# Q and k turned by VectorE blocks and SBUF moves instead of TensorE, with the row tiles in another order

## The reference

```
q, k = rmsnorm(xn @ Wq) * q_w, rmsnorm(xn @ Wk) * k_w      # per head, over its 128 columns
scores = q @ k.T / sqrt(128) - slope[h] * distance         # causal
y = rmsnorm(softmax(scores) @ v) * sub_w
out = x + concat(y) @ Wproj + fp8_roundtrip(xn) @ W8.T
```

## Time and profile before

| what | value |
|---|---|
| median of 3 runs (lowest to highest) | 547.68 us (547.47 to 548.8) |
| the profiled execution: its time, its span | 549.33 us, 547.2 us |
| TensorE matmul, busy | 521.6 us, 95% |
| VectorE, ScalarE, GpSimd, busy | 417.8, 391.6, 333.9 us |
| share of TensorE in the chain that ended last | 86% |
| mean of the DMA engines | 20 GB/s |

### The profile page before, as it was taken

One profiled execution on the slowest core, in us unless ns is written; L12 is line 12 of the kernel. 1 busy time (PEld: TensorE's weight loads), 2 busy tenths in 40 slices (PEclk: granted clock), 3 DMA queues, 4 the chain that ended last, 5 costly groups with the idle time before them and its releaser, 6 DMA issues.

```text
span 547.2 us, 11863 instructions
## 1 busy us (share of the span) xinstructions
PE 521.6 (95%) x3420; PEld 481.4 (88%) x3420; DVE 417.8 (76%) x1031; ACT 391.6 (72%) x887; POOL 333.9 (61%) x430
## 2 busy tenths in 40 slices
PE   6678999999999999999999999999999999999985
PEld 2667899999999999999999999999999999999874
DVE  5876768777787867878787777878678787868775
ACT  2367878686876968677696868768686877868662
POOL 3385587574758737676576748587376856747221
PEclk9699999999999999999999999999999999999999
DMA  5200100101010010101001010100101000000002
GB/s 158 58 2 1 40 1 1 40 2 40 2 38 0 0 38 0 38 0 38 0 1 37 0 38 0 38 0 9 30 0 38 0 10 0 10 2 1 2 1 77
DMA packets 18581, 10.81 MB, mean 20 GB/s; under 512 B 2176, under 2 KB 18560, under 8 KB 18560
## 3 DMA queue, kind: packets, MB, share of 16 engines
q1 hardware_dynamic: 17568, 10.49, 6.6%
q10 hardware_dynamic: 992, 0.07, 0.1%
HBM read 9.51 MB, written 1.05 MB: 19 GB/s over the span
## 4 chain that ended last, share of the span: by engine, by line
PE 86%; DVE 5%; ACT 4%; issue 2%; DMA 1%; POOL 1%; POOLq 0%; DVEq 0%; SPq 0%
PE pT_ps L562 11%; PE qkv_ps L477 10%; PE qkv_ps L479 8%; PE qkv_ps L478 8%; PE yT_ps L479 7%; PE yT_ps L478 7%; PE yT_ps L477 7%; PE score_big L477 5%; PE score_big L478 4%; PE score_big L479 4%; PE misc L538 3%; PE score_small L479 2%; PE score_small L478 2%; PE score_small L477 2%; ACT stage L734 1%
## 5 line engine op out<-in xcount | busy, mean ns | idle before, releaser
L919 DVE TENSOR_TENSOR pT_lo<-pT_ps,pT_hi 128x384 fp32r<-128x384 f32 (+1 forms) x192 | 101.0, 554 | 41.9 <-ACT pT_hi L762 41.2
L734 ACT ACTIVATE stage<-qkv_ps 128x384 f32<-128x384 f32 x119 | 58.5, 492 | 83.0 <-PE qkv_ps L479 82.3
L754 ACT ACTIVATE probs<-probs,neg_max 128x1024 f32<-128x1024 f32 (+7 forms) x128 | 98.4, 770 | 16.8 <-DVE neg_max L910 16.7
L762 ACT ACTIVATE pT_hi<-pT_ps 128x384 fp32r<-128x384 f32 (+1 forms) x192 | 86.2, 484 | 17.4 <-PE pT_ps L562 12.6
L431 POOL TENSOR_TENSOR y_r<-y_ms,minus_half 128x4 f32<-128x4 f32 x32 | 32.7, 1022 | 105.8 <-DVE y_ms L938 105.8
L477 PE MATMUL qkv_ps<-w_hi,xT_hi 128*128 128x384 f32 x242 | 87.9, 363 | 2.6 <-ACT stage L734 0.6
L562 PE MATMUL pT_ps<-ident,probs 128*128 128x128 f32 x576 | 84.5, 274 | 4.2 <-ACT probs L754 3.5
L478 PE MATMUL qkv_ps<-w_lo,xT_hi 128*128 128x384 f32 x242 | 82.0, 339 | 0.0
L479 PE MATMUL qkv_ps<-w_hi,xT_lo 128*128 128x384 f32 x242 | 81.9, 338 | 0.0
L391 POOL TENSOR_TENSOR qk_r<-qk_ms,minus_half 128x4 f32<-128x4 f32 x64 | 64.8, 1013 | 27.2 <-DVE qk_ms L884 25.6
L562 PEld LDWEIGHTS pT_ps<-ident,probs 128*128 128x128 f32 x576 | 66.3, 141 | 9.2 <-ACT probs L754 4.4
(11 more groups left out here) (183 smaller groups left out, 1313.3 us busy)
## 6 DMA issues: line engine op xcount, KB each, us to landing
w_raw<-in_wq SPq DMA_DIRECT2D x16, 128.0 KB, 2.2
w_raw<-in_wk SPq DMA_DIRECT2D x16, 128.0 KB, 2.3
w_raw<-in_wv SPq DMA_DIRECT2D x16, 128.0 KB, 2.3
wp_raw<-in_wproj SPq DMA_DIRECT2D x16, 128.0 KB, 2.1
acc<-in_x SPq DMA_DIRECT2D x2, 512.0 KB, 5.5
out<-acc SPq DMA_DIRECT2D x8, 128.0 KB, 1.8
w<-in_ffn_w ACTq DMA_DIRECT2D x1, 64.0 KB, 6.8
q_col<-in_q_w ACTq DMA_DIRECT2D x1, 0.5 KB, 2.9
```

Source lines behind the costliest of these rows:

```text
L734: act.activation(stage_of(h, k // 2)[:, k % 2, :], qkv_bank(h, k)[:, 0:3 * D], ACT.Copy).then_inc(qkv_read, 1)
L754: act.activation(probs[:, s % 2, 0:(i + 1) * P], probs[:, s % 2, 0:(i + 1) * P], ACT.Exp, bias=neg_max[:, par, s:s + 1], scale=-1.0, accum ...
L762: act.activation(pT_hi[g][:, a:b, r * P:(r + 1) * P], pT_ps[(CHUNK0[s] + k) % 2][:, 0:(b - a) * P].rearrange("p (j t) -> p j t", t=P), ACT ...
L919: dve.tensor_tensor(pT_lo[g][:, a:b, r * P:(r + 1) * P], pT_ps[(CHUNK0[s] + k) % 2][:, 0:(b - a) * P].rearrange("p (j t) -> p j t", t=P), ...
```

## The change: what it does

TensorE's `transpose_qk` goes for the heads 1 to 15. For each pair VectorE turns every 32x32 block of `qk_n` in place (`turn_blocks`, one instruction over 128x512, into `turned`), and SP moves the blocks to where a full transpose has them: 16 transfers within SBUF (`move_qk`), each 32 partitions by 128 columns (16 KB), into `qk_raw`. `qk_hi` and `qk_lo` then read `qk_raw` in SBUF rather than PSUM, and `qk_lo` has three instructions instead of two. `turned` and `qk_raw` have two buffers each: `turn_blocks` waits until the moves of two pairs ago have landed, and `move_qk` until `qk_lo` of two pairs ago is done. Head 0 still uses TensorE.

The row tiles go in the order 3, 4, 2, 5, 1, 6, 0, 7, so that a head's first score needs two of its four pairs, the second three, and only the sixth all (`NEEDS`). `qk_hi` and `qk_lo` of pair 3 move into step 1 of the head itself. The calls of all engines are placed anew: each `turn_blocks` stands one step or so behind its `mean_squares`, `qk_lo(k)` comes two or three steps later (turn 0, 1, 2, 3 in steps 1, 3, 5, 7; lo 0, 1, 2 in steps 4, 5, 7; lo 3 in step 1 of the next head); `project(h + 2, 0)` is pulled into the end of head h; GpSimd does `norm_qk` ahead of its weight splits. The far parts of `pT_hi` and `pT_lo` become narrower.

In the prologue x comes in four loads, `dist` is built before the normalization, `split_w(1, 1)` waits until x is normalized, ten more warm-up matmuls stand behind the first transposes, the first projections start with half of x, and the decoding of the fp8 weights is spread over the steps of head 0. The last head's closing calls are reordered.

```
-    ORDER = [7, 0, 6, 1, 5, 2, 4, 3]
+    ORDER = [3, 4, 2, 5, 1, 6, 0, 7]
...
+    WIDE = 4
+
+    NEEDS = [max(ORDER[:s + 1]) // 2 + 1 for s in range(NT)]
...
+            def move_qk(h, k):
+
+                m = NPAIR * (h - 1) + k
+                sp.wait_ge(blocks_turned, m + 1)
+                sp.nop(nofuse=True)
+                sp.wait_ge(qk_split, m + NPAIR - 1)
+                sp.nop(nofuse=True)
+                if isinstance(h, int) and h == 1 and k < 2:
+
+                    sp.wait_ge(v_split, NPAIR)
+                    sp.wait_ge(qk_normed, NPAIR)
+                for a in range(4):
+                    for b in range(4):
+                        sp.dma_start(qk_raw[32 * b:32 * b + 32, k % 2, a * P:(a + 1) * P],
+                                     turned[32 * a:32 * a + 32, k % 2, b * P:(b + 1) * P]).then_inc(qk_moved[k % 2], 16)
...
+                    for k in range(NPAIR):
+                        move_qk(h + 1, k)
...
-            def transpose_qk(h, par, k, now):
-                bank_free(now, f"qkT{k}")
-                pe.wait_ge(qk_normed, NPAIR * h + k + 1)
...
+                if s == 0 or NEEDS[s] > NEEDS[s - 1]:
+
+                    pe.wait_ge(qk_split, NPAIR * h + NEEDS[s])
...
+            pe.wait_ge(const_ready, 2)
+            warm(WARM_UP)
+            transpose_x(0)
+            transpose_x(1)
+            warm(KEEP_WARM)
+            for k in range(NT):
+                if k % 4 == 0:
+                    pe.wait_ge(xT_read, KT * (k // 4 + 1))
+                if k == NT - 1:
+                    transpose_first(0)
+                project(0, 0, k)
+                if k == 1:
+                    transpose_x(2)
+                    transpose_x(3)
+            transpose_first(1)
+            project(1, 1, 0)
+            score(0, 0, 0)
+            transpose_first(2)
+            project(1, 1, 1)
+            transpose_first(3)
+
             def head(h, par, tile, after):
...
             def qk_hi(h, par, k):
-                ps = first_ps(k) if isinstance(h, int) and h == 0 else job_ps(0, f"qkT{k}")
-                act.wait_ge(qkT_ready, NPAIR * h + k + 1)
+
+                act.wait_ge(qk_moved[k % 2], 256 * (2 * (h - 1) + k // 2 + 1))
                 at = slice(2 * k * P, (2 * k + 2) * P)
-                act.activation(qT_hi[:, par, at], ps[:, 0:2 * P], ACT.Copy, scale=q_col[:, 2:3])
-                act.activation(kT_hi[:, par, at], ps[:, 2 * P:4 * P], ACT.Copy).then_inc(qkT_hi_done, 1)
+                act.activation(by_block(qT_hi[:, par, at]), moved(k, 0), ACT.Copy, scale=q_col[:, 2:3])
+                act.activation(by_block(kT_hi[:, par, at]), moved(k, 1), ACT.Copy).then_inc(qkT_hi_done, 1)
...
+            def turn_blocks(h, k):
+
+                m = NPAIR * (h - 1) + k
+                dve.wait_ge(qk_normed, m + NPAIR + 1)
+                if isinstance(h, int) and h == 1 and k < 2:
+                    dve.wait_ge(v_split, NPAIR - 1)
+                past(dve, qk_moved[k % 2], 256 * (2 * (h - 1) + k // 2))
+                dve.nop(nofuse=True)
+                dve.transpose(turned[:, k % 2, :].rearrange("p (b n c) -> p b n c", b=4, n=4),
+                              qk_n[:, k % 2].rearrange("p t a (b c) -> p b (t a) c", b=4)).then_inc(blocks_turned, 1)
...
             def qk_lo(h, par, k):
-                ps = first_ps(k) if isinstance(h, int) and h == 0 else job_ps(0, f"qkT{k}")
+
                 dve.wait_ge(qkT_hi_done, NPAIR * h + k + 1)
                 at = slice(2 * k * P, (2 * k + 2) * P)
-                dve.scalar_tensor_tensor(qT_lo[:, par, at], ps[:, 0:2 * P], q_col[:, 2:3],
-                                         qT_hi[:, par, at].bitcast(f32), ALU.mult, ALU.subtract)
-                dve.tensor_tensor(kT_lo[:, par, at], ps[:, 2 * P:4 * P], kT_hi[:, par, at].bitcast(f32),
-                                  ALU.subtract).then_inc(misc_read, 1)
+                for t in range(2):
+                    dve.scalar_tensor_tensor(by_block(qT_lo[:, par, at])[:, t], moved(k, 0)[:, t], q_col[:, 2:3],
+                                             by_block(qT_hi[:, par, at].bitcast(f32))[:, t], ALU.mult, ALU.subtract)
+                dve.tensor_tensor(by_block(kT_lo[:, par, at]), moved(k, 1), by_block(kT_hi[:, par, at].bitcast(f32)),
+                                  ALU.subtract).then_inc(qk_split, 1)
 
             def mask(h, par, s):
```

GpSimd's order within a head:

```
             def head(h, par, tile, after):
...
+                if not last:
+                    norm_qk(h + 1, 0)
                 if not first:
                     norm_y(h - 1, 0)
                 if not last:
...
+                    split_v(h + 1, 1 - par, 0)
+                if has_head(h + 2):
+                    split_w(h + 2, par)
                 if not last:
...
+                    norm_qk(h + 1, 1)
+                    split_v(h + 1, 1 - par, 1)
+                    norm_qk(h + 1, 2)
+                    split_v(h + 1, 1 - par, 2)
                 if not first:
                     norm_y(h - 1, 1)
                 split_wp(h, par)
+                if not last:
+                    norm_qk(h + 1, 3)
+                    split_v(h + 1, 1 - par, 3)
```

More of the change, by code:

```diff
@@ L233, in build_block @@
         WARM_UP = 24
+        KEEP_WARM = 10
         def qkv_bank(h, k):
@@ new lines, in head @@
+                    if s == 0:
+                        if not first:
+                            probs_hi(h - 1, NT - 1)
+                            if not last:
+                                copy_qkv(h + 1, 0)
+                            exps(h, par, 0)
+                        exps(h, par, 1)
+                        if not last:
+                            if not first:
+                                copy_qkv(h + 1, 1)
+                            square_qk(h + 1, 0)
+                    if s == 1:
+                        if not first:
+                            square_y(h - 1, 0)
+                        probs_hi(h, 0)
+                        if not last:
+                            copy_qkv(h + 1, 2)
+                        if not first:
+                            qk_hi(h, par, 3)
+                        if isinstance(h, int) and h == 1:
+                            pass
@@ new lines, in head @@
+                    if s == 2:
+                        probs_hi(h, 1)
+                        if not first:
+                            y_out(h - 1, 1)
+                        exps(h, par, 2)
+                        if not last:
+                            copy_qkv(h + 1, 3)
+                            square_qk(h + 1, 1)
+                    if s == 3:
+                        if not last:
+                            copy_qkv(h + 1, 4)
+                        exps(h, par, 3)
+                        probs_hi(h, 2)
+                        if not last:
+                            copy_qkv(h + 1, 5)
+                            square_qk(h + 1, 2)
@@ new lines, in head @@
+                    if s == 4:
+                        probs_hi(h, 3)
+                        exps(h, par, 4)
+                        if not last:
+                            qk_hi(h + 1, 1 - par, 0)
+                            copy_qkv(h + 1, 6)
+                    if s == 5:
+                        if not first:
+                            square_y(h - 1, 1)
+                        exps(h, par, 5)
+                        probs_hi(h, 4)
+                        if not last:
+                            qk_hi(h + 1, 1 - par, 1)
+                            copy_qkv(h + 1, 7)
+                            square_qk(h + 1, 3)
```

604 lines of the change are left out of this document (311 added, 293 removed).

## The result

The changed kernel takes 756.33 us (754.18 to 759.06, four runs) against 547.92 for the kernel before (547.47 to 548.8): a ratio of 1.3803, interval 1.3754 to 1.3853. The forecast was 542, in a range of 521 to 562. It was wrong by 214 us, and on the other side.

The account below looks back on a forecast made before the run. TensorE was taken to bound the kernel before; after the change a loop through the moves would give 31.75 us per head. Heads +1.7, prologue -8.5 and end +1.5 us made -5.3, so 542 us, range 521 to 562.

Parts of the forecast that it names:

- The bounds of a step are 0.33 and 0.47 us. I take 0.38: SP's queue: time to issue one 32-row move, taken as 0.38 us from the trace's loads and stores.
- SP 64 x 0.38 + 4 x 0.46 = 26 us: SP's queue per head: 64 moves and four loads, 26 us, at the upper bound 31.9.
- the question of cover: Whether VectorE's work between `turn_blocks` and `qk_lo` hides 8.1 us; pair 1 falls 1.4 us short, pair 3 0.8.
- Rival 2: Slower: moves cost SP 0.43 us each and land after 1.8, period 32.8 us, 557 us in all; chance 0.28.
- The sum is 31.75 us: Loop from `turn_blocks(1)` to the next head's, through SP, ScalarE, VectorE and TensorE: period 31.75 us against 31.63.
- The reordering changes no column count: TensorE: the new row tile order was taken to leave the matmul columns unchanged; only 1.76 us of transposes leave per head.
- VectorE's load: VectorE's work per head was to grow from 24.31 to 27.1 us, with four turns at 0.6 and 0.4 more.
- the prologue: Start of the kernel: work begins at about 14.4 us, clock full from 14, first score near 28, 9.5 sooner.
- 8.5 us: Prologue's gain in the whole: 9.5 us at the first score less 1 for a projection; bounds 5 and 10.
- The landing, 1.8 us: Landing of a 16 KB move within SBUF, taken as 1.5 us, between 1.2 and 2.2.
- ScalarE does wait at `qT_hi`: Sign of the forecast: ScalarE waits for a transfer at `qT_hi`, some 2 to 4 us per head.
- 1.76 us of transposes: TensorE per head: sixteen transposes at 0.11 us leave its queue, allowing a period of 29.9 us.

Follow-up runs that it names:

- e1: Kernel before, with SP issuing series of extra unread transfers of different shapes in its second last head: 548.53 us.
- e12: Changed kernel with its 16 moves per pair and only the sum `add_out(h-1, 0, 1)` placed one step earlier on VectorE: 751.7 us.
- e2: Changed kernel with four moves of 128 partitions per pair instead of 16, blocks not exchanged, so q and k are wrong: 657.3 us.
- e4: Changed kernel, computing the same, with each pair's moves going through the chip's memory, one store and four loads instead of 16 transfers: 657.42 us.
- e7: e4 with the sum `add_out(h-1, 0, 1)` moved one step up on VectorE, from behind `mask(5)`: 601.3 us.
- e8: e7 with pair 2's split moved as well, `qk_hi(2)` into ScalarE's step 6 and `qk_lo(2)` to the start of step 7: 597.4 us.
- e5: Kernel before with only the row tile order changed to 3, 4, 2, 5, 1, 6, 0, 7: 567.5 us.
- e10: Changed kernel with the sum and pair 2's split placed early, without turns and moves, so q and k stay untransposed: 574.56 us.
- e11: Kernel before, with its row order and TensorE transposes, plus only the change's prologue: 546.12 us, ratio 0.9959.
- e9: Changed kernel with its 16 moves per pair and both the sum and pair 2's split placed early: 814.59 us.

## Why the prediction was wrong, step by step

**The step that failed: "The bounds of a step are 0.33 and 0.47 us. I take 0.38".** It is 0.633 us (e1, and 40.83 us for 64 in the changed kernel). I took the bounds from loads and stores and let the row count argue for less; the rows of before held no transfer with both sides in SBUF, and the kind, not the size, sets the price. "SP 64 x 0.38 + 4 x 0.46 = 26 us" is 40.8 + 1.9 us, with 1.5 us ahead of the first move and 0.2 behind the last: 44.5 in the head shown, 45.2 in the mean. With 0.633 even my own sum gives over 42 us, and the question of cover falls away: SP's queue is the bound, as e12 shows. Rival 2 named it ("SP's 31.9 us is a bound of its own") but at a price a quarter too low; its 0.43 us "as between neighbours of the trace" isn't in the rows either, which have 0.46 and 0.45. This step is 99 us (756.3 to 657.3, e2 to e4).

**The second: "The sum is 31.75 us".** Once the issues are few, the period should have been at or below that; it was 39.2 (e2). I followed one loop, through the moves, ScalarE and the scores, and took TensorE's stretch from score(1) to score(3) as free of waits, and the work after it as no concern. The loop that closed goes through a PSUM bank: `add_out(h-1, 0, 1)` on VectorE frees it for `turn_y(h-1, 1)` on TensorE. I had listed the sum in VectorE's cover at 0.87 us, and not asked who waits for it. It costs 56 us (e7), the place of pair 2's split 4 more (e8). The period of e8, 34.9 us (385.91 to 455.65 us, two heads), is still above my sum; that part stays open.

**The row order, priced at nothing.** "The reordering changes no column count" is true, and the order by itself costs 19 us (e5).

**VectorE's load.** `turned` took 0.706 us by itself, as I took it from its nearest rows. The rows of VectorE in the changed kernel (busy us, mean ns | idle before):

```profile
L967 DVE STREAM_TRANSPOSE turned<-qk_n 128x512 f32<-128x512 f32 x60 | 42.4, 706 | 8.7 <-POOL qk_n L211 7.2
...
L984 DVE SCALAR_TENSOR_TENSOR qT_lo<-qk_raw,q_col,qT_hi 128x128 fp32r<-128x128 f32 x120 | 40.9, 381 | 150.9 <-ACT kT_hi L780 150.3
...
L986 DVE TENSOR_TENSOR kT_lo<-qk_raw,kT_hi 128x256 fp32r<-128x256 f32 x60 | 35.3, 588 | 0.0
```

The two halves of `qT_lo` are 2 x 0.38 instead of 0.48 us, and `kT_lo` 0.59 instead of 0.42, so `qk_lo` costs 0.45 us per pair more in its records, where I had 0.1. VectorE has 28.2 us in that head and 29.4 in the mean with its neighbour, not 27.1. It is no bound by its sum, as said; what its load costs as a delay isn't parted from the trip (e10).

**Right:** the prologue. Projections start at 13.86 (walked: 14.4), the granted clock is 1.00 from 13.8 to 23.9 us, and the first score comes at 27.51 us (walked: 28):

```profile
13.86 0.44 PE L507 MATMUL qkv_ps<-w_hi,xT_hi 128*128 128x384 f32 x1 [0.74 <-DVE xT_lo L1070]
...
27.51 0.50 PE L507 MATMUL score_small<-kT_hi,qT_hi 128*128 128x512 f32 x1 [1.40 <-DVE kT_lo L976]
```

But "8.5 us" was counted as a gain of the whole, and e11 got 2.4 us at the end from 4.6 at the first score; whether the changed kernel, with tile 3 first, keeps more of it wasn't tried. The landing, 1.8 us, was inside my bounds. The 2.0 us that rival 2 took from the Trainium skill ("DMA: Bandwidth & Descriptors", Anatomy of one DMA) stand there for transfers that GpSimd issues, and these are SP's. ScalarE does wait at `qT_hi`, 14 us per head rather than 2 to 4.

**Of the 208 us**, 99 are SP's issues, 56 the place of one sum, 4 that of pair 2's split, 23 the turns and the remaining trip; 26 are left at e10's 574.6. The shares hold in this order of removal: with sixteen moves in place the sum is worth 4.6 us (e12), and the early split costs 63 (e9). The row order's 19, measured alone in the kernel before, may be most of them. That is an inference from two kernels, for the new order wasn't taken out of the changed one. Nor is it settled why none of the 1.76 us of transposes that TensorE loses per head shows: in e10 it waits 50 times for `pT_lo` (36.9 us), in the kernel before once (0.7 us), and which step of VectorE's order is late there stays open.

## What to carry to other kernels

Multiply each queue's issues by their price before asking whether a latency is hidden: a queue that only issues is an in-order engine like any other, and 64 issues at 0.63 us were more than the whole period. A price taken from a neighbouring row holds for the same kind of operation (here, the same pair of memories), not for the same size, and if no row has the kind, its upper bound is open. When calls are moved, list for each one who waits for what it frees, PSUM banks first; and measure a reordering by itself, for behind a larger bound an edit need not show what it is worth: 56 us became 4.6 (e12), and 4 us of gain became 63 of loss (e9).

## What the runs showed of the hardware

- SP issues a transfer with both sides in SBUF every 0.633 us, one with a side in HBM every 0.464, whatever its rows (32 or 128). Landing took 1.8 us for 16 KB. The Trainium skill ("DMA: Bandwidth & Descriptors", Rules for kernel authors) says that transfers under 64 KB cost mostly overhead. The runs agree: in e1 moves of 64 KB landed after 1.9 us, those of 16 KB after 1.8, and both cost the same issue. What set the period here was that issue, on the issuing queue.
- In e2 TensorE's granted clock was 1.00 during a wait of 2.76 us that ended at 321.32, 0.89 in the mean from 321.3 to 322.8, and 0.50 (1.2 GHz) from 322.8 to 325.9 us, where 512 columns took 0.42 instead of 0.25 us; from 325.9 it was 1.00 again. In the changed kernel the mean is 0.895, in e12 0.886, in e9 0.849.
- VectorE's subtraction with one operand in PSUM takes the same time wherever it stands, and with both in SBUF mostly longer, up to three times as long. The first row is of the kernel before, the second of e8 (ns min/median/max):

```profile
L893 DVE TENSOR_TENSOR kT_lo<-misc,kT_hi x46: 407/416/419, 32.6 to 507.1; 128x256 fp32r<-128x256 f32 x46
```

```profile
L988 DVE TENSOR_TENSOR kT_lo<-qk_raw,kT_hi x60: 412/612/1262, 52.1 to 564.8; 128x256 fp32r<-128x256 f32 x60
```

- In e8 the one at 391.94 us took 0.96 us beside GpSimd's `v_lo` from 391.76 to 392.62, also with two operands in SBUF. The Trainium skill ("SBUF — State Buffer", SBUF: two separate sides) describes a port pair that VectorE, with two SBUF inputs, and GpSimd hold in turn for a whole instruction; this trace fits that at this one place, and no run took GpSimd's work away.
